# Where the FFN's second bias is added: on GpSimd in the residual, or on TensorE by a matmul with a row of ones

## The chip, the cores and the metric

The kernel runs on one core of one Trainium2 chip. The metric is the device time of one execution in microseconds (us).

## The reference

The reference is a network of four residual parts over x, 16 batches of 256 tokens of 512 values: a long convolution with gating, a mixture of experts, an attention, and a plain FFN. Only the last one is touched:

```
x = x + _L1_ffn_ref(_layernorm(x), proj1, proj1_bias, proj2, proj2_bias, gate_w)
    h   = gelu(einsum('lne,he->lnh', x, proj1) + proj1_bias)      # 512 -> 2048
    out = einsum('lnh,eh->lne', h, proj2) + proj2_bias            # 2048 -> 512
```

The bias `proj2_bias` has 512 values, one for each output column, the same for all 4096 tokens.

## The kernel before

The program is a chain of three phases with a barrier between them: every engine of a phase first waits for all that the phase before has signalled. The first phase (tiles `c_` and `f_` in the trace) does the convolution and the experts, the second (`t_`) the attention, the third (`g_`, function `ffn_phase`) the last FFN. Within a phase each engine works through its own queue strictly in the order in which the program text puts instructions there; `p.do(engine, ..., waits)` adds one and returns a token, and a later instruction on any engine can wait for that token. SyncE (`sync`) issues the loads, GpSimd (`gpsimd`) the stores.

`ffn_phase` works on 8 groups G of 512 tokens (4 tiles t of 128 tokens), and for each group on 16 blocks k of 128 hidden values. All products are made from pairs of rounded parts: a value is split into a high part (`...h`) and a low part (`...l`) of type fp32r, and a product is three matmuls, high by high, low by high, high by low.

- At the start, the four tiles of group 0 are loaded (L986), then the two biases (L990, L991), then the first pair of weight blocks into the two staging buffers `stg` (`fetch(0, 0)`, L1090). `stats`, `norm` and `turn` make the layernorm of a tile (`bn_stats`, `bn_aggr`, a `tensor_scalar` on VectorE, a power on GpSimd, a `tensor_scalar` on VectorE) and transpose it on TensorE into `xh` and `xl`. `place_weights` splits the staged weights into `w1h`, `w1l`, `w2h`, `w2l`, on ScalarE and, for block 0, on GpSimd; later blocks use VectorE.
- `fetch` writes staging buffer i % 2 and waits for `st` and `sth` of i - 2, the two tokens that say that this buffer has been read.
- For each block, `first` makes 12 matmuls of 512 columns into `PH` (L1039), `hidden` the gelu on ScalarE (L1051) and the split into `hh` and `hl` on VectorE (L1052, L1053), and `second`, two blocks later, 12 matmuls of 512 columns (L1062): three for each of the four PSUM banks `O[t]`. A bank gathers over all 16 blocks of its group: the first matmul of block 0 has start=True, the last of block 15 stop=True. The pair `hh`, `hl` has two buffers, taken by the parity of the block.
- `raise_` adds the bias, held as 128 equal rows in `b2s`, to the residual tile `xt` on GpSimd (L1072), four times in a group, at blocks 5, 7, 9 and 11. `evac` then adds `O[t]` on VectorE (L1078) and stores the tile (L1079).
- `second` of block 0 of the next group waits, bank by bank, for that `evac`; `first` of a block stands between them in TensorE's queue.

The buffers of a phase are laid out in SBUF in the order of their `m.sb` calls.

Of the kernel before, what the change touches and what calls it, by code (L numbers as in the profile page):

```python
# [8 lines left out]
F32R = mybir.dt.float32r  # L9
I32 = mybir.dt.int32  # L10
U32 = mybir.dt.uint32
ALU = mybir.AluOpType
ACT = mybir.ActivationFunctionType
# [74 lines left out]
def f32(ap):  # L88
    return ap.bitcast(F32)
# [19 lines left out]
def make_identity(p, ident):  # L109
    a = p.do("gpsimd", lambda e: e.memset(ident, 0.0))  # L110
    return p.do("gpsimd", lambda e: e.affine_select(out=ident, in_=ident, compare_op=ALU.not_equal, fill=1.0, base=0,
                                                    pattern=[[-1, 128]], channel_multiplier=1), a)
# [832 lines left out]
def ffn_phase(nc, ctx, d, before, tag, xin, accs, outs, passes, w1, w2, b1, brow):  # L945
# [3 lines left out]
    NG = 8  # L949
    groups = NG * len(passes)  # L950
    p = Phase(nc, ctx, tag, before)
    m = Mem(nc, ctx, tag)
# [7 lines left out]
    b1s = m.sb("b1s", list(b1.shape))  # L960
    stg = m.sb("stg", [128, 2, 512])

    b2s = m.sb("b2s", [128, 512])
    xt = m.sb("xt", [128, 2, 4, 512])
    ac = m.sb("ac", [128, 4, 512]) if len(passes) > 1 else None
    st = m.sb("st", [128, 2, 6])
    ag = m.sb("ag", [128, 2, 2])
    rs = m.sb("rs", [128, 2, 1])
    xn = m.sb("xn", [128, 2, 512])
# [5 lines left out]
    O = [m.ps(f"O{i}") for i in range(4)]  # L975
    PH = [m.ps(f"PH{i}") for i in range(2)]
    PM = m.ps("PM")
    T = {}

    def g(*k):  # L980
        return T.get(k)
# [4 lines left out]
        T["x0", i] = p.dma("sync", dx0[i], lambda e, i=i: e.dma_start(xt[:, 0, i, :], xin[0][:, i, :]))  # L986
    c_id = make_identity(p, ident)
    c_mh = p.do("gpsimd", lambda e: e.memset(mhalf, -0.5))
    db = p.dsem("bias")
    p.dma("sync", db, lambda e: e.dma_start(b1s[:, :], b1))  # L990
    c_b = p.dma("sync", db, lambda e: e.dma_start(b2s[:, :], brow))  # L991

    da = p.dsem("a")
    dw = [p.dsem(f"w{i}") for i in range(2)]
# [59 lines left out]

    def second(G, k):
        n = G * NB + k
        for t in range(4):
            c = slice(128 * t, 128 * t + 128)
            for q, (a, b_) in enumerate(((hh, w2h), (hl, w2h), (hh, w2l))):
                fin = k == NB - 1 and q == 2  # L1060
                beg = k == 0 and q == 0
                tk = p.do("tensor", lambda e, a=a, b_=b_, t=t, fin=fin, c=c, beg=beg: e.matmul(O[t][:, :], a[:, n % 2, c], b_[:, k, :], start=beg, stop=fin),  # L1062
                          g("hh", n), g("hl", n), g("w2", k), g("add", 4 * (G - 1) + t) if k == 0 else None, inc=(q == 2 and (t == 3 or fin)))
                if fin:
                    T["o", 4 * G + t] = tk
                if q == 2 and t == 3:
                    T["o2", n] = tk

    def raise_(G, t):
        i = 4 * G + t  # L1070
        x = xt[:, G % 2, t, :]
        T["xb", i] = p.do("gpsimd", lambda e: e.tensor_tensor(x, x, b2s[:, :], ALU.add), c_b, g("xn", i))  # L1072

    def evac(G, t):
        i = 4 * G + t
        x = xt[:, G % 2, t, :]
        r = x if G < NG else ac[:, t, :]
        T["add", i] = p.do("vector", lambda e: e.tensor_tensor(x, r, O[t][:, :], ALU.add), g("o", i), g("xb", i))  # L1078
        T["out", i] = p.dma("gpsimd", dout[i % 8], lambda e: e.dma_start(outs[G // NG][G % NG][:, t, :], x), g("add", i))  # L1079

    nst = [0]
# [1 line left out]
    def fetch(G, k):  # L1083

        kb = passes[G // NG][k]
        for src in (w1[kb], w2[kb]):
            i = nst[0]
            nst[0] += 1
            q = stg[:, i % 2, :]
            T["wd", i] = p.dma("sync", dw[i % 2], lambda e, q=q, src=src: e.dma_start(q, src), g("st", i - 2), g("sth", i - 2))  # L1090

    def place_weights(G, k, eng="vector"):

        free = g("o2", (G - 1) * NB + k) if G else None
        i = nst[0] - 2
        ws = ((w1h[:, k, :, :].rearrange("p a b -> p (a b)"), w1l[:, k, :, :].rearrange("p a b -> p (a b)")), (w2h[:, k, :], w2l[:, k, :]))
        for j, (hi, lo) in enumerate(ws):
            T["sth", i + j], T["st", i + j] = split_weight(p, stg[:, (i + j) % 2, :], hi, lo, T["wd", i + j], free, eng)
        T["w1", k], T["w2", k] = T["st", i], T["st", i + 1]
# [30 lines left out]
    for n in range(total + 2):  # L1130
        G, k = divmod(n, NB)
        if n < total:
            if G == 0 and k + 1 < NB:
                place_weights(0, k + 1)
                if k + 2 < NB:
                    fetch(0, k + 2)
            prepare(G, k, 0)
            first(G, k)
            prepare(G, k, 1)
        if n >= 2:  # L1140
            G2, k2 = divmod(n - 2, NB)
            second(G2, k2)
            if (G2 + 1) % NG == 0 and G2 + 1 < groups:

                if k2:
                    place_weights(G2 + 1, k2 - 1)
                fetch(G2 + 1, k2)
                if k2 == NB - 1:
                    place_weights(G2 + 1, k2)
            if k2 in (5, 7, 9, 11):  # L1150
                raise_(G2, (k2 - 5) // 2)
            if k2 == NB - 1:
                for t in range(4):
                    evac(G2, t)
                if G2 + 2 < groups:
                    load(G2 + 2)
                if G2 + 1 < groups:
                    load_acc(G2 + 1)
        if n < total:
            hidden(G, k)  # L1160
# [484 lines left out]
def layouts(inputs):  # L1645

    i = {k: np.asarray(v) for k, v in inputs.items()}
    c = np.ascontiguousarray
    a = {"x": c(i["x"]), "ctx": c(i["ctx_2048"]), "k": c(np.pad(i["L0_xattn_k"], ((0, 0), (128, 0))))}
    ctx = i["ctx_2048"]  # L1650
    a["ctxh"] = c(ctx.reshape(16, 32, 8, 4, 128).transpose(1, 4, 3, 0, 2).reshape(32, 128, 4, 128))
    a["ctxb"] = c(ctx.reshape(16, 256, 4, 128).transpose(0, 3, 2, 1))
    a["skipt"] = c(np.tile(i["fside_S2_0"].reshape(32, 8).T, (16, 1)))
    a["seg"] = c(i["itok_BxS_0_1023"].reshape(16, 2, 128).transpose(0, 2, 1))
    a["rw1"] = c(i["L0_ffn_w1"].reshape(8, 4, 128, 256).transpose(0, 2, 1, 3).reshape(8, 128, 2, 512).transpose(0, 2, 1, 3).reshape(16, 128, 512))
    a["rw2"] = c(i["L0_ffn_w2"].reshape(16, 128, 512))
    a["sw1"] = c(i["L0_ffn_shared_w1"].reshape(4, 128, 4, 128).transpose(2, 1, 0, 3).reshape(4, 128, 512))
    a["sw2"] = c(i["L0_ffn_shared_w2"].reshape(4, 128, 512))
    a["sb1"] = c(i["L0_ffn_shared_b1"].reshape(4, 128).T)
    a["rb1"] = c(i["L0_ffn_b1"])  # L1660
    b2 = np.zeros((96, 512), np.float32)
    for z in (0, 32, 64):
        b2[z:z + 9] = np.concatenate([i["L0_ffn_b2"], i["L0_ffn_shared_b2"][None]])
    a["f0b2"] = b2[:73]
    a["gw"] = c(i["L0_ffn_gate_w"].reshape(4, 128, 8).transpose(1, 0, 2))
    a["f1w1"] = c(i["L1_ffn_proj1"].T.reshape(4, 128, 16, 128).transpose(2, 1, 0, 3).reshape(16, 128, 512))
    a["f1w2"] = c(i["L1_ffn_proj2"].T.reshape(16, 128, 512))
    a["f1b1"] = c(i["L1_ffn_proj1_bias"].reshape(16, 128).T)
    a["f1b2"] = c(np.tile(i["L1_ffn_proj2_bias"], (128, 1)))
    uq, qr, dq, kr = i["L1_xattn_W_uq"], i["L1_xattn_W_qr"], i["L1_xattn_W_dq"], i["L1_xattn_W_kr"]  # L1670
    uqt = uq.T.reshape(16, 128, 192)
    ukt, uvt = [i["L1_xattn_" + n].T.reshape(16, 128, 128) for n in ("W_uk", "W_uv")]
    a["fac"] = c(np.concatenate([uqt, uqt[:, :, 128:], ukt, uvt, i["L1_xattn_W_o"].reshape(16, 128, 512)], -1))
    a["wqra"] = c(qr[:128])
    a["wqrb"] = c(np.concatenate([qr[128:], qr[128:]]))
    a["wkc"] = c(i["L1_xattn_W_kvc"].reshape(4, 128, 128).transpose(1, 0, 2))
    a["wdq"] = c(np.concatenate([dq, dq[:, 128:]], 1).reshape(4, 128, 256).transpose(1, 0, 2))
    sw = np.concatenate([kr[:, 32:], kr[:, :32]], 1)
    a["wkr"] = c(np.stack([np.concatenate([kr, kr], 1), np.concatenate([sw, sw], 1)], 1))
    inv = np.float32(1.0) / np.float32(10000.0) ** (np.arange(32, dtype=np.float32) / np.float32(32))  # L1680
    ang = np.arange(256, dtype=np.float32)[:, None] * inv
    co, si = np.cos(ang).astype(np.float32), np.sin(ang).astype(np.float32)
    co, si = np.concatenate([co, co], 1), np.concatenate([-si, si], 1)
    a["ck"], a["sk"] = c(np.tile(co.T, (2, 1))), c(np.tile(si.T, (2, 1)))
    a["cq"], a["sq"] = c(co.reshape(2, 128, 64).transpose(1, 0, 2)), c(si.reshape(2, 128, 64).transpose(1, 0, 2))
    return a
# [55 lines left out]
```

How the kernel before makes its waits and increments, by code:

```python
    def emit(self, e, eng):  # L69
        seen = {}
        def wait(sem, v):
            if seen.get(id(sem), 0) < v:
                eng.wait_ge(sem, v)
                seen[id(sem)] = v
        for sem, v in self.before:
            wait(sem, v)
        for fn, waits, inc in self.q[e]:
            for w in waits:
                if w is not None:
                    wait(*w)
            ins = fn(eng)
            if inc:
                ins.then_inc(*inc)
# [1635 lines left out]
                def run(eng, e=e):  # L1721
                    for p in phases:
                        p.emit(e, eng)
                    if e == "sync":
                        for sem, v in before:
                            eng.wait_ge(sem, v)
```

## Time and profile before

| | |
|---|---|
| median of 3 runs | 3286.62 us (3286.21 to 3289.66) |
| the profiled execution, one of the three | 3289.66 us |
| its span, first to last instruction | 3287.9 us |
| outside the span | 1.76 us |
| phase 3 in the span | from about 2539 us to the end |
| TensorE busy, whole span | 97% |
| granted TensorE clock, mean | 0.989 of full |

In the profile, L12 means line 12 of the kernel; PE is TensorE, PEld its weight loads, DVE VectorE, ACT ScalarE, POOL GpSimd, SPq the queue of SyncE. A row of the timeline gives the start of an instruction (us from the span's start) and its length. Matmuls are pipelined, so a matmul's length is longer than its distance to the next: what TensorE spends on each is read from start to start.

### The profile page before, as it was taken

Reading aid. Unit: us, or ns where it says so; the run is one execution under the profiler, and the core shown is the slowest. Engines: PE = TensorE matmul, PEld = TensorE weight load, DVE = VectorE, ACT = ScalarE, POOL = GpSimd, SP = SyncE. Lnnn points to the kernel's source line nnn. Section 1 sums busy time; section 2 is a strip of 40 time slices with the busy share of each in tenths; the row PEclk is TensorE's granted clock in tenths of the full one; section 3 lists DMA queues with packets and bytes.
Section 4 is the critical chain, followed back from the end, with each engine's and each line's share of the span. In section 5 each row is a group of like instructions: output and inputs, shape, how many; then the busy total and the mean of one; then the engine's idle time right before and its main releaser. Section 6 shows DMA issues by size and latency. Waiting matters only on the chain.

```text
span 3287.9 us, 51710 instructions
## 1 busy us (share of the span) xinstructions
PE 3176.7 (97%) x18581; PEld 2696.9 (82%) x18581; DVE 2174.6 (66%) x5816; ACT 1267.6 (39%) x3058; POOL 1052.6 (32%) x1114
## 2 busy tenths in 40 slices
PE   7999999999999789999999999999998999999999
PEld 4666666688899679999999999999997788888887
DVE  6888888755555477787878777777876533333332
ACT  2333333233444255555555555555554411111111
POOL 6877777535211222222222222222200111010110
PEclk9999999999999899999999999999999999999999
DMA  4544443259644432111111111111101300000000
GB/s 130 156 135 139 128 143 91 81 168 313 197 152 155 158 116 71 46 46 46 40 40 44 46 46 44 37 45 46 46 14 43 109 26 26 26 26 26 26 14 13
DMA packets 123764, 267.41 MB, mean 81 GB/s; under 512 B 17673, under 2 KB 18321, under 8 KB 123514
## 3 DMA queue, kind: packets, MB, share of 16 engines
q1 hardware_dynamic: 100122, 186.59, 18.1%
q0 software_dynamic: 23392, 77.51, 7.1%
q8 instruction: 153, 2.51, 0.3%
q14 instruction: 97, 0.79, 0.1%
HBM read 159.49 MB, written 104.56 MB: 80 GB/s over the span
## 4 chain that ended last, share of the span: by engine, by line
PE 78%; DVE 10%; POOL 7%; DMA 2%; ACT 1%; issue 1%; SPq 0%; POOLq 0%; DVEq 0%
PE g_PH L1039 11%; PE g_O L1062 11%; PE t_U L1505 10%; PE t_S L1457 9%; PE t_PO L1492 5%; PE t_M L1441 5%; POOL c_kf L354 3%; PE t_T L1479 3%; PE f_Y L916 3%; PE f_Y L386 2%; PE t_M L1396 2%; PE f_Y L687 2%; PE f_Y L381 2%; DVE c_R L399 2%; DVE c_z L393 2%; PE t_M L1378 2%
## 5 line engine op out<-in xcount | busy, mean ns | idle before, releaser
L1467 ACT ACTIVATE t_pr<-t_sm,t_nb 128x256 f32<-128x256 f32 x512 | 256.4, 502 | 369.2 <-DVE t_nb L1463 369.2
L1052 DVE CAST g_hh<-g_hf 128x512 fp32r<-128x512 f32 x128 | 61.8, 482 | 431.4 <-PE g_O L1062 426.8
L1411 POOL TENSOR_TENSOR t_r<-t_r 128x256 f32<-128x256 f32 x128 | 95.7, 748 | 776.0 <-DVE t_rw L1473 457.6
L354 POOL TENSOR_TENSOR c_kf<-c_vt,c_ct 128x512 f32<-128x512 f32 x256 | 296.6, 1179 | 0.2 <-PE f_Y L381 0.2
L1051 ACT ACTIVATE g_hf<-g_PH,g_b1s 128x512 f32<-128x512 f32 x128 | 88.2, 689 | 514.5 <-PE g_PH L1039 514.5
L1474 DVE TENSOR_SCALAR t_pr<-t_pr,t_rw 128x256 f32<-128x256 f32 x512 | 222.2, 434 | 18.2
L386 PE MATMUL f_Y<-c_kh,c_th 128*128 128x512 f32 x448 | 201.1, 449 | 9.2 <-ACT c_kh L361 9.2
L1039 PE MATMUL g_PH<-g_xh,g_w1h 128*128 128x512 f32 x512 | 205.3, 401 | 1.5 <-DVE g_xl L1027 1.5
L1039 PE MATMUL g_PH<-g_xh,g_w1l 128*128 128x512 f32 x512 | 202.9, 396 | 0.0
L1039 PE MATMUL g_PH<-g_xl,g_w1h 128*128 128x512 f32 x512 | 202.6, 396 | 0.0
L1062 PE MATMUL g_O<-g_w2h,g_hh 128*128 128x512 f32 x512 | 202.4, 395 | 0.0
L1505 PE MATMUL t_U<-t_vol,t_oth 128*128 128x512 f32 x512 | 202.3, 395 | 0.0
L1062 PE MATMUL g_O<-g_w2h,g_hl 128*128 128x512 f32 x512 | 202.2, 395 | 0.0
L1505 PE MATMUL t_U<-t_voh,t_otl 128*128 128x512 f32 x512 | 202.0, 395 | 0.0
L1062 PE MATMUL g_O<-g_w2l,g_hh 128*128 128x512 f32 x512 | 201.5, 394 | 0.0
L1505 PE MATMUL t_U<-t_voh,t_oth 128*128 128x512 f32 x512 | 200.9, 392 | 0.0
L1463 DVE CUSTOM_DVE_ANT_0 t_sm<-t_S,t_mk 128x256 f32<-128x256 f32 x512 | 194.8, 418 | 7.7 <-PE t_S L1457 7.7
L393 DVE TENSOR_TENSOR c_z<-f_Y,c_ct 128x512 f32<-128x512 f32 x256 | 174.1, 680 | 37.2 <-PE f_Y L381 37.0
L381 PE MATMUL f_Y<-c_kf,c_t 128*128 128x512 f32 x384 | 186.4, 594 | 0.0
L1484 DVE TENSOR_TENSOR t_ptl<-t_T,t_pth 128x512 fp32r<-128x512 f32 x256 | 175.6, 686 | 15.5 <-ACT t_pth L1483 15.4
L399 DVE TENSOR_REDUCE c_R<-c_z 128x64 f32<-128x512 f32 x256 | 175.0, 683 | 6.6
L386 PE MATMUL f_Y<-c_kh,c_tl 128*128 128x512 f32 x448 | 178.2, 398 | 0.0
(355 smaller groups left out, 9695.1 us busy)
## 6 DMA issues: line engine op xcount, KB each, us to landing
xs<-c_zero SPq DMA_DIRECT2D x71, 256.0 KB, 5.2
f_xg<-xs SPq DMA_DIRECT2D x71, 256.0 KB, 2.8
ys<-f_yt POOLq DMA_DIRECT2D x71, 256.0 KB, 2.4
c_tr<-kpad SPq DMA_DIRECT2D x60, 256.0 KB, 4.8
f_xg<-xn SPq DMA_DIRECT2D x40, 256.0 KB
c_xt<-x SPq DMA_DIRECT2D x32, 256.0 KB, 3.5
c_cr<-ctx SPq DMA_DIRECT2D x32, 256.0 KB, 3.9
c_ct<-ctxh SPq DMA_DIRECT2D x32, 256.0 KB, 4.3
```

Of the source, the lines that this page charges most:

```text
L354: T["kv", h] = T["kv1", n] = p.do("gpsimd", lambda e: e.tensor_tensor(o, iv, ic, ALU.mult), g("vt", h), g("ct", h), g("kl", n - 8), g("kh" ...
L381: last = p.do("tensor", lambda e, c=c, mb=mb: e.matmul(Y[y % 4][:, :], t0[:, s, c], kf[:, v, mb, :], start=False, stop=mb == lb), g("t0", ...
L386: last = p.do("tensor", lambda e, a=a, b_=b_, c=c, mb=mb, i=i: e.matmul(Y[y % 4][:, :], a[:, s, c], b_[:, v, mb, :], start=(mb == 0 and i ...
L393: T["z", h] = T["z1", y] = p.do("vector", lambda e: e.tensor_tensor(zz.rearrange("p (b j i) -> p b j i", i=8, j=8), iv, ic, ALU.mult), las ...
L399: T["red", y] = T["R", h] = p.do("vector", lambda e: e.tensor_reduce(rr, zr, AXX, ALU.add), g("z1", y), g("pr", h - 2))
L1039: T["ph", n] = p.do("tensor", lambda e, kk=kk, a=a, b_=b_, i=i: e.matmul(ph[:, :], a[:, k, kk, :], b_[:, s, kk, :], start=i == 0, stop=i = ...
L1062: tk = p.do("tensor", lambda e, a=a, b_=b_, t=t, fin=fin, c=c, beg=beg: e.matmul(O[t][:, :], a[:, n % 2, c], b_[:, k, :], start=beg, stop= ...
L1457: a = p.do("tensor", lambda e, t=t, j=j, q=q, k=k: e.matmul(PS1[:, 256 * t:256 * t + 256], q, k[:, s, :], start=j == 0, stop=j == 4), g("q ...
L1463: T["am", N] = am = p.do("vector", lambda e, t=t, k4=k4: e.tensor_tensor_reduce(out=sm[:, k4, :], in0=PS1[:, 256 * t:256 * t + 256], in1=m ...
L1467: T["ex", x] = p.do("scalar", lambda e, t=t, k4=k4: e.activation(pr[:, N % 2, t, :], sm[:, k4, :], ACT.Exp, bias=nb[:, k4, 0:1], scale=-1. ...
L1474: T["nm", x] = p.do("vector", lambda e, t=t, k4=k4: e.tensor_scalar(pr[:, N % 2, t, :], pr[:, N % 2, t, :], rw[:, k4, 1:2], None, ALU.mult ...
L1505: a = p.do("tensor", lambda e, t=t, tt=tt, j=j, o=o, w=w: e.matmul(PU[t][:, :], o[:, N % 3, tt], w[:, h, :], start=h == 0 and j == 0, stop ...
```

## The change

The bias leaves the residual. It becomes one more matmul in front of each PSUM bank's sum: the stationary operand is `oner` (33 rows by 128 columns, ones in rows 0 and 32, zeros between), the moving operand `br` (33 rows by 512 columns, row 0 the bias's high part, row 32 its low part). The host now hands over 33 rows, zeros but for rows 0 and 32, instead of 128 equal rows. They are loaded into the first staging buffer, rounded to fp32r on ScalarE (`c_bh`), and row 32 is replaced by the remainder on VectorE (`c_br`). As the staging buffer is shared with the weights, the tokens of these two become `sth` and `st` of index -2, on which the first `fetch` waits. `oner` is made by three memsets on GpSimd and a copy on VectorE. The four adds of `raise_` in a group go, and `evac` waits for what `raise_` had waited for.

```diff
-    b2s = m.sb("b2s", [128, 512])
+    KB = 33
+    BL = slice(32, 33)
+    brs = stg[0:KB, 0, :]
+    br = m.sb("br", [KB, 512], F32R)
...
+    ones = m.sb("ones", [33, 128])[:, :]
+    oner = m.sb("oner", [33, 128], F32R)[:, :]
+    a = p.do("gpsimd", lambda e: e.memset(ones, 0.0))
+    for z in (0, 32):
+        a = p.do("gpsimd", lambda e, z=z: e.memset(ones[z:z + 1, :], 1.0), a)
+    c_on = p.do("vector", lambda e: e.tensor_copy(oner, ones), a)
     db = p.dsem("bias")
     p.dma("sync", db, lambda e: e.dma_start(b1s[:, :], b1))
-    c_b = p.dma("sync", db, lambda e: e.dma_start(b2s[:, :], brow))
+    c_b = p.dma("sync", db, lambda e: e.dma_start(brs, brow))
+    c_bh = p.do("scalar", lambda e: e.activation(br[:, :], brs, ACT.Copy), c_b)
+    c_br = p.do("vector", lambda e: e.tensor_tensor(br[BL, :], brs[BL, :], f32(br[BL, :]), ALU.subtract), c_bh, c_b)
+    T["sth", -2], T["st", -2] = c_bh, c_br
...
     def second(G, k):
         n = G * NB + k
+        bias = G // NG == len(passes) - 1
         for t in range(4):
             c = slice(128 * t, 128 * t + 128)
+            if k == 0 and bias:
+
+                p.do("tensor", lambda e, t=t: e.matmul(O[t][:, :], oner, br[:, :], start=True, stop=False),
+                     c_on, c_br, g("add", 4 * (G - 1) + t), inc=False)
             for q, (a, b_) in enumerate(((hh, w2h), (hl, w2h), (hh, w2l))):
                 fin = k == NB - 1 and q == 2
-                beg = k == 0 and q == 0
+                beg = k == 0 and q == 0 and not bias
...
-    def raise_(G, t):
-        i = 4 * G + t
-        x = xt[:, G % 2, t, :]
-        T["xb", i] = p.do("gpsimd", lambda e: e.tensor_tensor(x, x, b2s[:, :], ALU.add), c_b, g("xn", i))
-
     def evac(G, t):
...
-        T["add", i] = p.do("vector", lambda e: e.tensor_tensor(x, r, O[t][:, :], ALU.add), g("o", i), g("xb", i))
+        T["add", i] = p.do("vector", lambda e: e.tensor_tensor(x, r, O[t][:, :], ALU.add), g("o", i), g("x", G), g("a", G), g("xn", i))
...
-            if k2 in (5, 7, 9, 11):
-                raise_(G2, (k2 - 5) // 2)
...
-    a["f1b2"] = c(np.tile(i["L1_ffn_proj2_bias"], (128, 1)))
+    b2 = np.zeros((33, 512), np.float32)
+    b2[0], b2[32] = i["L1_ffn_proj2_bias"], i["L1_ffn_proj2_bias"]
+    a["f1b2"] = b2
```

## Rows read from the trace of the kernel before

**Rows 1.** Stretches of the last phase: us, busy and count per engine, PEclk, DMA share, GB/s.
```profile
2534.00:2554.03 20.03, 4.85 (x19) 3.12 (x19) 10.86 (x23) 4.14 (x8) 6.36 (x10) 0.57 0.50 170
2554.03:3282.25 728.22, 728.22 (x3184) 589.04 (x3184) 252.19 (x457) 123.57 (x186) 72.51 (x90) 1.00 0.09 30
```

**Rows 2.** Timeline of TensorE, two `second` blocks: start, length, instruction.
```profile
2564.04 0.40 PE L1062 MATMUL g_O<-g_w2h,g_hh 128*128 128x512 f32 x1
...
2566.80 0.39 PE L1039 MATMUL g_PH<-g_xh,g_w1h 128*128 128x512 f32 x1
...
2569.60 0.40 PE L1062 MATMUL g_O<-g_w2h,g_hh 128*128 128x512 f32 x1
...
2572.40 0.39 PE L1039 MATMUL g_PH<-g_xh,g_w1h 128*128 128x512 f32 x1
```

**Rows 3.** Tile g_xt: the adds that the change removes; length ns min/median/max.
```profile
L1072 POOL TENSOR_TENSOR g_xt<-g_xt,g_b2s x32: 1275/1293/1464, 2594.4 to 3204.1; 128x512 f32<-128x512 f32 x32
```

**Rows 4.** Who waited for whom from 2600 us on: us in total, times, longest.
```profile
DVE g_xt L1078 <- PE g_O L1062: 18.1, 8, 2.3
```

**Rows 5.** Timeline, phase 1: a matmul with 73 rows of contraction between ones with 128.
```profile
864.16 0.39 PE L687 MATMUL f_Y<-c_sw,f_hh 128*128 128x512 f32 x1
864.39 0.40 PE L683 MATMUL f_Y<-f_br,f_gT 73*128 73x512 f32 x1
864.63 0.39 PE L687 MATMUL f_Y<-c_sw,f_hh 128*128 128x512 f32 x1
```

**Rows 6.** The chain that ended last, at the last phase's start: start, length, what.
```profile
2539.61 2.68 DMA g_xt<-x
...
2542.41 0.70 DVE g_st L117
...
2554.03 10.17 PE g_PH L1039 x36
```

**Rows 7.** Timeline of the last phase's start, all engines.
```profile
2539.61 1.76 SPq L986 DMA_DIRECT2D g_xt<-x  x4
...
2541.41 0.43 SPq L990 DMA_DIRECT2D g_b1s<-f1b  x1
2541.88 0.43 SPq L991 DMA_DIRECT2D g_b2s<-f1b  x1
2542.36 8.31 SPq L1090 DMA_DIRECT2D g_stg<-f1w  x4
...
2546.91 0.62 ACT L105 ACTIVATE g_w1h<-g_stg 128x512 fp32r<-128x512 f32 x1
...
2552.61 0.60 ACT L1026 ACTIVATE g_xh<-g_O 128x512 fp32r<-128x512 f32 x1 [1.64 <-PE g_O L1021]
...
2553.24 0.69 DVE L1027 TENSOR_TENSOR g_xl<-g_O,g_xh 128x512 fp32r<-128x512 f32 x1 [1.24 <-ACT g_xh L1026]
```

**Rows 8.** DMA issues of that start: KB each, us to landing.
```profile
g_xt<-x SPq DMA_DIRECT2D x1, 256.0 KB, 4.4
g_b2s<-f1b SPq DMA_DIRECT2D x1, 256.0 KB, 4.1
g_stg<-f1w SPq DMA_DIRECT2D x1, 256.0 KB, 4.3
g_b1s<-f1b SPq DMA_DIRECT2D x1, 8.0 KB, 3.7
```

**Rows 9.** Timeline, phase 1: the same kind of bias split, and a copy to fp32r.
```profile
19.12 0.63 ACT L422 ACTIVATE f_br<-f_stg 73x512 fp32r<-73x512 f32 x1 [3.13 <-DMA f_stg<-f0b]
...
20.13 0.68 DVE L423 TENSOR_TENSOR f_br<-f_stg,f_br 9x512 fp32r<-9x512 f32 x1
...
22.16 0.23 DVE L428 CAST c_one<-c_onef 128x128 fp32r<-128x128 f32 x1 [1.36 <-POOL c_onef L427]
```

**Rows 10.** Timeline of TensorE before and where its granted clock rises in this phase.
```profile
2556.73 0.63 PE L1039 MATMUL g_PH<-g_xh,g_w1h 128*128 128x512 f32 x1
2557.16 0.48 PE L1039 MATMUL g_PH<-g_xh,g_w1l 128*128 128x512 f32 x1
```

## The prediction

> **What bounds the kernel now.** I read the page's busy shares first: TensorE is busy 97% of the span, which is an average over three phases and says little of this one. The change lives in the last phase alone, so I read the stretches of that phase. From its first block matmul at 2554.03 us to its last one at 3282.25 us TensorE is busy for all of 728.22 us, with 3184 matmuls, while VectorE is busy for 252 us, ScalarE for 124 and GpSimd for 73 [rows 1]. That is busy time by modelled ends, so I checked it start to start. 3072 of the 3184 are block matmuls of 512 columns, 112 are transposes. One group of twelve takes 2566.80 - 2564.04 = 2.76 us, another 2572.40 - 2569.60 = 2.80 us [rows 2], so a matmul costs 0.230 or 0.233 us of TensorE's time, although each row gives it a length near 0.39. 3072 x 0.232 = 713 us; the remaining 15 us are 28 sets of four transposes (about 0.45 each, 13 us) and a slow beginning, and that is the whole stretch. There is no stall left in it: TensorE sets the end, and each matmul put into its queue there moves the end by its start-to-start time.
>
> The other place where this phase can lose time is its start. From 2534.00 to 2554.03 us TensorE is busy for 4.85 us of 20.03 at half its clock (PEclk 0.57) [rows 1]. There the chain that ended last leaves TensorE: it runs from the load of the first tile over the first `bn_stats` at 2542.41, VectorE's and GpSimd's small steps, and transposes to the first block matmul at 2554.03 [rows 6]. What delays VectorE there delays everything.
>
> **The change part by part.**
>
> *Removed adds.* 32 adds on GpSimd of 1.293 us each (41 us) go [rows 3]. GpSimd has 72.5 us of work in 728 [rows 1], and the only instruction behind the adds, `evac`'s add on VectorE, idles for TensorE's last matmul of a bank and for nothing else (18.1 us, 8 times) [rows 4]. Gain on the path: 0. If this cover were gone, by GpSimd being late, the row of waits would name GpSimd; it doesn't.
>
> *Added matmuls.* Eight groups times four banks are 32 matmuls with 512 columns and 33 rows of contraction, each with its weight load. This phase has no such shape. Phase 1 has one with 73 rows between matmuls of 128 rows: 864.39 - 864.16 = 0.23 us before it and 864.63 - 864.39 = 0.24 behind it [rows 5]. It costs what a full matmul costs; fewer rows save nothing, and the change of shape loses nothing. 32 x 0.233 = 7.5 us. The bounds: in proportion to the rows, 33/128 of that, 1.9 us; or the full shown length, 0.396 each (the row says 0.40), 12.7 us, if the pipeline drained at each. I take 7.5, since row 864.39 is nearly the same thing. The waits of these matmuls cost nothing: `oner` and `br` are ready some 20 us earlier, and the wait for the add on the same bank is the one that the first matmul of a bank had, covered by the 2.8 us of `first` in front of it.
>
> The Trainium skill's page "TensorE: Matmul & The Clock Gate", section "Back-to-back issue gap", gives a sustained spacing of about 131 ns for a matmul of 512 columns in a stream with weight loads; this trace shows 233 ns in the same kind of stream, with fp32r operands. By the skill's figure the 32 would cost an estimated 4.2 us and the whole change an estimated 8.4; the row decides.
>
> *The start.* This is what I think is easily missed. `c_br`, the subtraction that makes the bias's low part, stands in VectorE's queue ahead of `stats(0)`, and it waits for `c_bh` on ScalarE, which waits for the bias's load. Queues are in order, so the first `bn_stats`, which could begin at 2542.41 because its tile had landed at 2542.29 (2539.61 + 2.68) [rows 6], now stands behind the bias. Before, nothing at the start waited for the bias: its first reader was the gelu.
> When does the bias land? The loads are issued in order: the four tiles, b1s at 2541.41, the bias at 2541.88, the weights at 2542.36 [rows 7]. The last of the four tiles, issued at about 2539.61 + 1.76 - 0.43 = 2540.9 [rows 7], took 4.4 us and landed at about 2545.3; b1s landed at 2541.41 + 3.7 = 2545.1, the bias of 256 KB at 2541.88 + 4.1 = 2546.0 [rows 8]. The new one is 33 rows of 2 KB, 66 KB, behind the same megabyte of tiles; `c_b` counts both biases. I take 2545.2, near b1s; bounds 2544.2 (if the tiles land a microsecond earlier because no weights follow close behind) and 2546.0 (no earlier than the large one).
> Then `c_bh`: 0.63 us, as for the 73-row bias [rows 9]; about 0.03 us from ScalarE's end to VectorE's start, as from 2552.61 + 0.60 to 2553.24 [rows 7]; `c_br`: 0.68 us, as for 9 rows [rows 9]; and 0.05 us to the first `bn_stats`, together 1.4 us. So `bn_stats` begins at 2546.6 instead of 2542.41: 4.2 us later. Bounds: 2544.2 + 1.4 gives 3.2; 2546.0 + 1.4 and a slower hand-over (in phase 1 VectorE began 20.13 - 19.75 = 0.38 us after ScalarE had ended [rows 9]) give 5.4.
> Do the weights become a second delay? SyncE holds `fetch(0, 0)` until `c_br` has ended, since it writes the same staging buffer, and with it everything behind it in SyncE's queue: both weight blocks, `fetch(0, 1)` and the next group's tile load. Before, the fetch was issued at 2542.36, 0.05 us before the first `bn_stats`, and ScalarE first used a weight block 4.5 us after that `bn_stats`, at 2546.91 [rows 7], when it had just landed (2542.36 + 4.3) [rows 8]. After, it is issued at the same moment relative to `bn_stats`, with no tiles ahead of it, so it lands no later relative to the chain. Both shift together: no extra cost. Without that cover the ScalarE queue, in which the next tile's `xh` stands behind the weights, would pass it on one for one.
> The three memsets on GpSimd fall into its idle time before the first `rs`, and the copy of 33 x 128 on VectorE (a 128 x 128 one took 0.23 us [rows 9]) into VectorE's idle time until the tile or the bias lands: 0.
> The rise of the clock moves along with the stream. At 2556.73 matmuls are 0.43 us apart, and the fast level (2.4 GHz for 1.2) comes at about 2557.3, some 3.3 us into the dense stream [rows 10]. Relative to the stream it may come earlier or later by chance: 8 matmuls at the slow level cost 8 x 0.2 = 1.6 us now, so I allow 1.5 us either way and expect 0.
>
> *Elsewhere.* `br` takes the place of `b2s` (2 KB in each partition both) and `oner` comes behind all other buffers, so no other buffer moves. The end behind 3282.25 is unchanged.
>
> *Sum.* 0 + 7.5 + 4.2 = 11.7 us. The profiled execution took 3289.66 us (span 3287.9 and 1.76 outside), so such an execution would take 3301.4. It was the slowest of three and lies 3.04 us above their median; against the median of 3286.62 the forecast is 3298.3 us, 0.36% slower. No change that can be measured means within 0.2% of the median, 6.6 us: 3280.0 to 3293.2.
>
> **Rivals.**
>
> *The start is free.* The bias would land early enough, or other work would catch up the delay before 2554.03. For it: VectorE idles in that start. Against: no block of idle time follows the first `bn_stats`, where the chain runs almost without a wait [rows 6]. It gives 3286.62 + 7.5 = 3294.1, hardly slower than the bound.
>
> *Each odd-shaped matmul drains the pipeline.* Then 12.7 + 4.2 = 16.9 us, 3303.5. Against it, the 0.24 us behind the 73-row matmul [rows 5].
>
> *Few rows are cheap.* 1.9 + 4.2 = 6.1 us, 3292.7, no measurable change. The same row speaks against it.
>
> *The added matmuls slip in at a lower spacing.* By the distance that a fully pipelined stream would allow, if the added ones, which all load the same 33 rows and stream the same `br`, ran at half of the present 0.233 us: 3.7 + 4.2 = 7.9 us, 3294.5. Against: in 728 us of stream the mean never falls there, and the groups of twelve in [rows 2], three to a bank, show 0.230 at the least. The Trainium skill's spacing of about 131 ns, cited above, is the rule that stands beside this case.
>
> *The other side: the stream itself gets faster.* Of the groups of twelve some take 2.76 us, others 2.80, and in `second` this goes by the parity of the block, so by which buffer of `hh` and `hl` is read [rows 2]. If the change moved buffers or access patterns so that the 128 groups of `first` and the 64 slow ones of `second` all ran at 2.76, it would give back 192 x 0.035 = 6.7 us: 11.7 - 6.7 = 5.0, 3291.6, not slower by my bound. It decides from 5.1 us of 6.7 on. Against: the buffers stay where they are.
>
> **How the numbers follow.** The forecast 0.75; free start 0.10; drain 0.05; cheap rows 0.03; lower spacing 0.03; faster stream 0.04. Bounds of the forecast's own terms: 7.4 + 3.2 - 1.5 = 9.1 and 7.5 + 5.4 + 1.5 = 14.4, 3295.7 to 3301.0. Runs of the same kernel spread by 3.5 us, so I widen to 3302.0 above. Below, the range takes in the free start and the lower spacing, 3293.5. Slower by over 0.2%: the forecast, drain, lower spacing and half of the free start, 0.88. Within: the other half, cheap rows and three quarters of the faster stream, 0.11. Faster: 0.01.
>
> **What the profile after would show.** 3216 matmuls in the stream, 32 of them with the form 33 x 512 and their next start 0.23 us on; VectorE's `bn_stats` beginning about 4.2 us later than before, with a wait for ScalarE in front of `c_br`, and the first block matmul about as much later; the first weight load issued behind it; no GpSimd adds; `evac`'s wait still for TensorE. I would be wrong if the barrier of the phase or the tiles' landing shifted too, if the row of the 33-row matmul showed 0.4 us to its next, or if the odd and even groups of twelve no longer took 2.80 and 2.76.

## The result, and the profile after

The changed kernel takes 3311.16 us (median of 6 runs, 3310.03 to 3315.59) against 3286.36 us (6 runs, 3285.16 to 3289.66) before: ratio 1.0075, 95% interval 1.0064 to 1.0086. It is slower by 24.8 us. The forecast was 3298.3 us, 11.7 us more than before, with a range to 3302.0: the sign was right, the size was half of the real one.

The profiled execution of the changed kernel is not one of these six; it took 3308.17 us, with a span of 3306.4. That is 18.5 us more than the profiled one before, not 24.8, because in it the two earlier phases, whose code is the same, ended 5.8 us sooner: the first tile load of the last phase was issued at 2533.80 us instead of 2539.61 [rows 7]. Measured from that load to the end of the span, the last phase took 3287.9 - 2539.61 = 748.3 us before and 3306.4 - 2533.80 = 772.6 us after. The difference, 24.3 us, is the one of the medians, and this is the measure to compare profiles by here. That the two agree within half a microsecond is partly chance: the start alone varies by more than that from profile to profile, as the experiments show.

First the stretches of the last phase, the start and the stream of block matmuls (us, busy and count of PE, PEld, DVE, ACT, POOL, then PEclk, DMA share, GB/s), as in [rows 1]:

```profile
2533.40:2552.93 19.53, 4.17 (x16) 2.92 (x17) 10.41 (x23) 4.77 (x9) 6.14 (x12) 0.50 0.44 138
2552.93:3301.00 748.07, 747.96 (x3216) 592.68 (x3216) 238.69 (x458) 123.84 (x186) 32.34 (x58) 1.00 0.09 29
```

The stream has its 32 more matmuls, 3216, and all but 0.1 us of it is busy by this view, at full clock. It begins at 2552.93 and its last matmul starts at 3300.49, 747.56 us later; before, from 2554.03 to 3282.02, it was 727.99 (the prediction's 3282.25 is the end of its stretch). So 19.6 us of the 24.3 came in the stream. Divided by 32 this is 0.61 us for each added matmul, where I had put down 0.233.

The timeline of TensorE and its weight loads around one of them, the second bias matmul of a group:

```profile
2657.90 0.40 PE L1079 MATMUL g_O<-g_w2l,g_hh 128*128 128x512 f32 x1
2658.23 0.18 PEld L1074 LDWEIGHTS g_O<-g_br,g_oner 33*128 33x128 f32 x1 [0.36 <-issue]
2658.23 0.50 PE L1074 MATMUL g_O<-g_br,g_oner 33*128 33x512 f32 x1
2658.65 0.19 PEld L1079 LDWEIGHTS g_O<-g_w2h,g_hh 128*128 128x128 f32 x1 [0.24 <-issue]
2658.66 0.50 PE L1079 MATMUL g_O<-g_w2h,g_hh 128*128 128x512 f32 x1
2658.76 0.19 PEld L1079 LDWEIGHTS g_O<-g_w2h,g_hl 128*128 128x128 f32 x1
2659.00 0.39 PE L1079 MATMUL g_O<-g_w2h,g_hl 128*128 128x512 f32 x1
```

Read the PE rows from start to start: 0.33 us from the matmul before to the bias matmul, 0.43 to the next, 0.34 to the one behind that, and then 0.23 again. Now read the PEld rows. Elsewhere in the stream a weight load begins together with the matmul before it and is over when that ends. Here the bias's weight load begins only with its own matmul, 0.33 us after the one before had begun, and so does the load behind it. Two loads in a row have lost their cover, and the third, at 2658.76, begins 0.10 us later than the matmul that should cover it. The means over all 32 are 0.326, 0.427 and 0.34 us, 1.09 us for three distances, of which two were there before: the price is 1.09 - 2 x 0.232 = 0.63 us, 32 x 0.63 = 20.2 us. The stream grew by 19.6, a little less, and two small things lie between: the clock rose about 0.4 us later in this execution (below), and of the undisturbed groups of twelve in `second` only 38 of 117 took 2.80 us instead of 2.76, where before it was 61 of 125, which gives back about 0.8 us.

The matmul's own length is 0.497 us, by the view of the tile g_br (min/median/max in ns), but a sum made from the lengths would not have found 0.63 either, because a part of it falls on the neighbours:

```profile
L1074 PE MATMUL g_O<-g_br,g_oner x32: 492/497/498, 2563.5 to 3221.7; 33*128 33x512 f32 x32
```

The start, in the chain that ended last (start, length, what):

```profile
2536.08 3.81 DMA g_stg<-f1b
...
2540.00 0.64 ACT g_br L1001
2540.66 0.68 DVE g_br L1002
2541.37 0.71 DVE g_st L117
...
2552.93 10.60 PE g_PH L1051 x36
```

In [rows 6] the chain went from the tile's load straight to `g_st L117`. Now it goes through the bias's load, `c_bh` (L1001) and `c_br` (L1002). The first `bn_stats` begins 2541.37 - 2533.80 = 7.57 us behind the first tile load, before 2542.41 - 2539.61 = 2.80: 4.8 us later. The first block matmul begins 19.13 us behind that load, before 14.42: 4.7 us later.

The removed adds: `evac`'s wait for TensorE is the same as in [rows 4].

```profile
DVE g_xt L1090 <- PE g_O L1079: 18.1, 8, 2.3
```

### The profile page after: what moved, and what is told of

Same layout as the page of the kernel before. It is cut to its first block, busy times and chain, and to the rows that moved or that the text cites. A ratio compares the mean times of both kernels' runs of the same rounds, so it can differ in the third digit from the quotient of the medians.

```text
span 3306.4 us, 51716 instructions
## 1 busy us (share of the span) xinstructions
PE 3190.9 (97%) x18613; PEld 2698.1 (82%) x18613; DVE 2164.9 (65%) x5818; ACT 1269.4 (38%) x3059; POOL 1014.3 (31%) x1085
## 4 chain that ended last, share of the span: by engine, by line
PE 79%; DVE 10%; POOL 7%; ACT 1%; DMA 1%; issue 1%; SPq 0%; POOLq 0%; DVEq 0%; ACTq 0%
PE g_PH L1051 11%; PE g_O L1079 11%; PE t_U L1515 10%; PE t_S L1467 9%; PE t_PO L1502 5%; PE t_M L1451 5%; POOL c_kf L354 3%; PE t_T L1489 3%; PE f_Y L916 3%; PE f_Y L687 2%; PE f_Y L386 2%; PE t_M L1406 2%; PE f_Y L381 2%; DVE c_R L399 2%; DVE c_z L393 2%; PE t_M L1388 2%
## 5 line engine op out<-in xcount | busy, mean ns | idle before, releaser
L1064 DVE CAST g_hh<-g_hf 128x512 fp32r<-128x512 f32 x128 | 55.0, 429 | 481.8 <-PE g_O L1079 476.8
```

## The experiments

The two theories that I took into them. For the stream: the shape of the new matmul is at fault (A), or its place in front of a bank and its waits (B). For the start: the bias's split at the head of VectorE's queue, or something else in the set-up. The times below come from two later sessions, each with the kernel before on the same chip: 3286.97 us for the runs "65 rows", "four together", "start alone" and "split moved", 3286.42 us for "64 rows", "32 rows", "adds alone" and "both repairs". The ratios are taken within a session. Where a run is set against the changed kernel's 3311.16 us, measured with 3286.36 us before, the comparison crosses sessions, and up to 0.6 us of it is the sessions' own difference.

**65 rows instead of 33.**

```diff
-    KB = 33
-    BL = slice(32, 33)
+    KB = 65
+    BL = slice(64, 65)
```

with `ones`, `oner` and the host's array of 65 rows to match, ones and bias in rows 0 and 64.

> The bias matmul with 65 rows of contraction instead of 33 (ones in rows 0 and 64, the low part in row 64, zeros between); nothing else. Theory A (shape): at 64 rows or fewer the array works in a narrower arrangement, and going into and out of it costs 0.63 us per bias matmul; 65 rows behave like the 73 rows of the first phase: 0.23 us to the next start, weight load under the matmul before, so 32 x (0.63 - 0.23) = 12.8 us off the changed kernel, about 3298.4 us. Rival B (place): it is dear because it opens a PSUM bank or because of its waits, whatever its rows: it stays at 0.33 + 0.43 us and the time at about 3311.

3298.69 us (5 runs), ratio 1.0039, interval 1.0025 to 1.0053. Theory A, to 0.3 us; 12.5 us below the changed kernel. The profiles say the same of the stream, from the first block matmul to the last: 735.4 us against 747.6. The timeline around a bias matmul:

```profile
2659.71 0.40 PE L1051 MATMUL g_PH<-g_xl,g_w1h 128*128 128x512 f32 x1
2659.72 0.19 PEld L1074 LDWEIGHTS g_O<-g_br,g_oner 65*128 65x128 f32 x1
2659.95 0.40 PE L1074 MATMUL g_O<-g_br,g_oner 65*128 65x512 f32 x1
2659.95 0.19 PEld L1079 LDWEIGHTS g_O<-g_w2h,g_hh 128*128 128x128 f32 x1
...
2660.18 0.40 PE L1079 MATMUL g_O<-g_w2h,g_hh 128*128 128x512 f32 x1
```

Both weight loads lie under the matmul before them again, and the distances are 0.24 and 0.23 us. The matmul stands at the same place, opens the same bank and has the same waits: B falls.

**64 rows.** The same edit with 64 rows, ones and bias in rows 0 and 32.

> The bias matmul with 64 rows (ones in rows 0 and 32, zeros between and behind). Theory A puts the border between 64 and 65 rows: 0.33 us before and 0.43 behind each bias matmul, as with 33 rows. If the cost grew smoothly as rows fall, or had to do with 33 as an odd number, 64 rows would show 0.23 or something between; one run, about 3311 against about 3299.

3313.48 us in one run.

```profile
2661.91 0.40 PE L1051 MATMUL g_PH<-g_xl,g_w1h 128*128 128x512 f32 x1
2662.23 0.18 PEld L1074 LDWEIGHTS g_O<-g_br,g_oner 64*128 64x128 f32 x1 [0.37 <-issue]
2662.24 0.49 PE L1074 MATMUL g_O<-g_br,g_oner 64*128 64x512 f32 x1
...
2662.66 0.19 PEld L1079 LDWEIGHTS g_O<-g_w2h,g_hh 128*128 128x128 f32 x1 [0.24 <-issue]
```

0.33 and 0.42 us, as with 33 rows; the means over the 32 are 0.326 and 0.427. Between 64 rows and 65 there is a step, not a slope. The single total, 2.3 us above the changed kernel's median, says no more than that; the distances carry the reading.

**32 rows.** One one, the high part alone, no subtraction.

```diff
-    KB = 33
+    KB = 32
...
-    c_br = p.do("vector", lambda e: e.tensor_tensor(br[BL, :], brs[BL, :], f32(br[BL, :]), ALU.subtract), c_bh, c_b)
+    c_br = c_bh
```

> The bias matmul with 32 rows: only row 0 holds a one and the bias's high part; the low part and its subtraction on VectorE are left out. By theory A the same price as with 33 rows or near it: the stream leaves the 128-row arrangement just the same, 0.33 and 0.43 us. If the narrowest shape were cheaper, its distance to the next would be under 0.43. The start is some 0.7 us shorter for want of the subtraction: about 3310.5 by theory A.

3304.23 us in one run, where 3310.5 was expected. The distances are what A says:

```profile
2655.03 0.50 PE L1073 MATMUL g_O<-g_br,g_oner 32*128 32x512 f32 x1
2655.46 0.19 PEld L1078 LDWEIGHTS g_O<-g_w2h,g_hh 128*128 128x128 f32 x1 [0.24 <-issue]
```

0.43 us to the next, and a mean of 0.425 over the 32. The stream takes 747.4 us, as in the changed kernel. The total lies 6 us lower than expected, and part of that is the start, which I had misjudged. Without the subtraction nothing at the head of VectorE's queue waits for the bias any more:

```profile
2532.07 1.76 SPq L988 DMA_DIRECT2D g_xt<-x  x4
...
2534.70 0.69 DVE L117 BATCH_NORM_STATS2 g_st<-g_xt 128x6 f32<-128x512 f32 x1 [1.01 <-DMA g_xt<-x]
...
2538.35 0.63 ACT L1000 ACTIVATE g_br<-g_stg 32x512 fp32r<-32x512 f32 x1 [13.51 <-DMA g_stg<-f1b]
...
2539.01 6.24 SPq L1101 DMA_DIRECT2D g_stg<-f1w  x4
...
2541.68 0.63 ACT L105 ACTIVATE g_w1h<-g_stg 128x512 fp32r<-128x512 f32 x1 [2.22 <-DMA g_stg<-f1w]
```

The first `bn_stats` is back at 2.63 us behind the first tile load, and what is late now is the weight fetch (L1101), which still waits for `c_bh`. ScalarE waits 2.22 us for those weights, and the chain that ended last goes from there over the low parts on GpSimd to the first block matmul, 2548.61 - 2532.07 = 16.5 us behind the load: 2.6 us sooner than in the changed kernel, 2.1 us later than before. From the first load to the end it took 3301.9 - 2532.07 = 769.8 us against 772.6, which is this difference. So the bias holds up two queues side by side; the fetch alone would cost 2.1 us, and in the changed kernel it is hidden behind the late `bn_stats`. The rest of the 6 us lies ahead of this phase, in one execution: its first tile load was issued at 2532.07 us, sooner than in any other profile.

**The four bias matmuls of a group together.**

```diff
+        for t in range(4 if k == 0 and bias else 0):
+            p.do("tensor", lambda e, t=t: e.matmul(O[t][:, :], oner, br[:, :], start=True, stop=False),
+                 c_on, c_br, g("add", 4 * (G - 1) + t), inc=False)
         for t in range(4):
             c = slice(128 * t, 128 * t + 128)
-            if k == 0 and bias:
-
-                p.do("tensor", lambda e, t=t: e.matmul(O[t][:, :], oner, br[:, :], start=True, stop=False),
-                     c_on, c_br, g("add", 4 * (G - 1) + t), inc=False)
```

> The four bias matmuls of a group stand one behind the other ahead of the twelve others of block 0 instead of one ahead of each three; 33 rows as before. Theory A1 (only the switch costs): one way in and one way out per group instead of four; the three inner distances fall from 0.43 to 0.23 us; 8 x (4 x 0.63 - (0.09 + 3 x 0.23 + 0.43 + 0.11)) = 9.6 us off, about 3301.6. Theory A2 (the narrow matmul itself streams at half rate): inner distances 0.43, 8 x (2.52 - (0.09 + 4 x 0.43 + 0.11)) = 4.8 us off, about 3306.4. Rival B (the bank's opening costs): no gain, 3311.

3300.72 us (4 runs), ratio 1.0047, interval 1.0030 to 1.0063: 10.4 us off the changed kernel, A1 had said 9.6, A2 4.8. The stream takes 737.4 us, 10.1 less. In the timeline the four are one row:

```profile
2656.86 0.40 PE L1051 MATMUL g_PH<-g_xl,g_w1h 128*128 128x512 f32 x1
2657.18 1.20 PE L1071 MATMUL g_O<-g_br,g_oner 33*128 33x512 f32 x4
2658.31 0.50 PE L1078 MATMUL g_O<-g_w2h,g_hh 128*128 128x512 f32 x1
2658.65 0.40 PE L1078 MATMUL g_O<-g_w2h,g_hl 128*128 128x512 f32 x1
```

Narrower windows of the same timeline leave out the first of the four, the first two, the first three, and so show where the others start; below them are the weight loads behind the four:

```profile
2657.52 0.86 PE L1071 MATMUL g_O<-g_br,g_oner 33*128 33x512 f32 x3
2657.75 0.62 PE L1071 MATMUL g_O<-g_br,g_oner 33*128 33x512 f32 x2
2657.99 0.39 PE L1071 MATMUL g_O<-g_br,g_oner 33*128 33x512 f32 x1
...
2658.31 0.19 PEld L1078 LDWEIGHTS g_O<-g_w2h,g_hh 128*128 128x128 f32 x1 [0.37 <-issue]
2658.42 0.19 PEld L1078 LDWEIGHTS g_O<-g_w2h,g_hl 128*128 128x128 f32 x1
```

The distances are 0.32 into the new shape, then 0.34, 0.23, 0.24, then 0.32 back to 128 rows and 0.34 behind that. Over all eight groups the means are 0.327, 0.340, 0.232, 0.232, 0.323 and 0.342. So a matmul of 33 rows isn't slow: between its like it is 0.23 us apart, the speed of the 128-row stream. What costs is each change of shape, and it costs at two places, about 0.09 us at the first matmul of the new shape, whose weights load only with it, and about 0.11 at the second, whose weights load 0.11 us late. The 0.43 us behind a lone bias matmul is both at once, the second place of the way in and the first of the way out: 0.232 + 0.11 + 0.09. One visit costs 0.32 + 1.13 + 0.34 - 2 x 0.232 = 1.33 us with four matmuls in it, of which 4 x 0.233 = 0.93 is their own time: 0.40 us for a way in and out, as for a lone matmul, 0.63 - 0.23.

**The start alone.** The changed kernel without its bias matmuls; the bias is not added.

```diff
-            if k == 0 and bias:
-
-                p.do("tensor", lambda e, t=t: e.matmul(O[t][:, :], oner, br[:, :], start=True, stop=False),
-                     c_on, c_br, g("add", 4 * (G - 1) + t), inc=False)
...
-                beg = k == 0 and q == 0 and not bias
+                beg = k == 0 and q == 0
```

> The bias matmuls are left out (the bias is then not added at all); the split at the start, the shared staging buffer and the removed adds stay as in the changed kernel. It shows the start's price alone. If the start costs 4.7 us (the profile after has the first block matmul that much later behind the first load) and the removed adds give nothing: 3286.4 + 4.7 = 3291.1. If the removed adds on GpSimd give TensorE something back, less. If the start is free: 3286.4.

3291.51 us (10 runs), ratio 1.0015, interval 1.0005 to 1.0025: 4.5 us for the start, as expected, though the interval alone would allow anything from 1.6 to 8.2. The profile is narrower: from the first tile load to the end 3289.3 - 2537.08 = 752.2 us against 748.3 before, 3.9 us, with the first block matmul 18.5 us behind the load instead of 14.4. Among the profiles with the split at the head of the queue (33, 64 and 65 rows, four together, and this one) that delay lies between 4.1 and 5.4 us.

**The split moved behind the first block.**

```diff
-    brs = stg[0:KB, 0, :]
...
+    brs = m.sb("brs", [KB, 512])[:, :]
...
-    c_bh = p.do("scalar", lambda e: e.activation(br[:, :], brs, ACT.Copy), c_b)
-    c_br = p.do("vector", lambda e: e.tensor_tensor(br[BL, :], brs[BL, :], f32(br[BL, :]), ALU.subtract), c_bh, c_b)
-    T["sth", -2], T["st", -2] = c_bh, c_br
...
+        if n == 0:
+            c_bh = p.do("scalar", lambda e: e.activation(br[:, :], brs, ACT.Copy), c_b)
+            c_br = p.do("vector", lambda e: e.tensor_tensor(br[BL, :], brs[BL, :], f32(br[BL, :]), ALU.subtract), c_bh, c_b)
         if n < total:
             hidden(G, k)
```

The new staging buffer lies behind all others, and the split stands between the first block's matmuls and its gelu.

> The bias gets a staging buffer of its own behind all others, and its split on ScalarE and VectorE stands behind the first block instead of ahead of the layernorm; the weight fetch no longer waits for it. 33 rows and all 32 bias matmuls stay. My theory (VectorE's and SyncE's queues held up by the bias): the first bn_stats begins again 2.8 us behind the first load, and 4.7 us go, about 3306.5. Rival (the start is later for another reason, such as the tiles' landing or the additional set-up work): the start stays 19.1 us from the first load to the first block matmul and the time stays at 3311.

3306.62 us (4 runs), ratio 1.0063, interval 1.0046 to 1.0080: 4.5 us off the changed kernel. The timeline of its start:

```profile
2536.72 1.76 SPq L988 DMA_DIRECT2D g_xt<-x  x4
2538.52 0.43 SPq L999 DMA_DIRECT2D g_b1s<-f1b  x1
2539.00 0.39 SPq L1000 DMA_DIRECT2D g_brs<-f1b  x1
...
2539.45 0.69 DVE L117 BATCH_NORM_STATS2 g_st<-g_xt 128x6 f32<-128x512 f32 x1 [0.85 <-DMA g_xt<-x]
...
2551.20 0.77 PE L1048 MATMUL g_PH<-g_xh,g_w1h 128*128 128x512 f32 x1 [1.46 <-DVE g_xl L1036]
```

`bn_stats` waits for its tile again and begins 2.73 us behind the first load (2.80 before); the first block matmul 14.48 us behind it (14.42 before). The memsets and the copy for `oner` are still there, so they cost nothing. This edit frees the weight fetch too, so it removes both of the waits that the run with 32 rows tells apart.

**The removed adds alone.** As the one above, and no bias matmuls; the bias is not added.

> Only the 32 adds on GpSimd are gone: no bias matmuls, and the split of the bias stands behind the first block with a staging buffer of its own (the bias is not added at all). My step: the adds were covered by TensorE's work and their removal gives 0: 3286.7, ratio 1.000. Rival: GpSimd's traffic slowed VectorE or TensorE, and its removal gives back some us: under 3283.

3287.21 us (11 runs), ratio 1.0004, interval 0.9995 to 1.0013. No difference that can be seen; the interval leaves room for a gain of 1.6 us and a loss of 4.3. The profile closes it further: from the first tile load to the end it is 3285.5 - 2537.33 = 748.2 us, against 748.3 with the adds. The adds were covered.

**Both repairs.** 65 rows and the late split.

> The change with both repairs: 65 rows of contraction, and the split of the bias behind the first block with its own staging buffer. Left is the plain price of 32 matmuls at 0.233 us: 3286.7 + 7.5 = 3294.2, ratio 1.0023. If the two repairs shared a cause, more than that would remain; if the removed adds gave something back, less.

3293.75 us (11 runs), ratio 1.0023, interval 1.0014 to 1.0032. This is the idea of the change at its plain price, 7.3 us above the kernel before by these medians, where 32 x 0.233 = 7.5 was expected; the interval is 4.6 to 10.5. In the profile the stream takes 736.4 us, 8.4 more than before, and 0.9 of that lies in its first 36 matmuls, among which the clock rose later (10.9 us against 10.0), so 7.5 are left. It doesn't beat the kernel before, and nothing in these runs points to a version that would: the work taken away is worth nothing, and TensorE has no gap to put a matmul in.

## Why the prediction was wrong

- *TensorE sets the end; each matmul put into its queue moves it.* Right. Of the changed kernel's 24.8 us 12.5 go with the shape, 4.5 with the split, and what is left, 7.8, is about the 7.3 of the kernel with both repairs. By the differences within each session it is 13.1, 5.1 and 6.6, so the shares are good to about a microsecond.
- *Removed adds: 0.* Right on the path, shown by the run without adds and matmuls. VectorE did lose time to them, which the wait of `evac` doesn't show (last section).
- *Added matmuls: 7.5 us.* This is the step that failed: "It costs what a full matmul costs; fewer rows save nothing, and the change of shape loses nothing", and "I take 7.5, since row 864.39 is nearly the same thing". The first half is right: in a row of four, the third and the fourth 33-row matmul each start 0.23 us behind the one before. The second is wrong. A 73-row matmul between 128-row ones [rows 5] is not a nearby case of a 33-row one: between 64 and 65 rows lies a step, and 73 is on the side of 128. The term measured 32 x 0.63 = 20.2 us. I should have asked which property of a shape makes its neighbours' weight loads fit under it, and not by how many rows it differed.
  The upper bound was too low for a second reason. I took the shown length, 0.396 us, as the most that a drained pipeline could cost; 12.7 us. But the price falls on three distances, and two of them end in matmuls that aren't new: the successor, whose weights load only with it, and the one behind that, whose weights load late. The rival "each odd-shaped matmul drains the pipeline" was the right mechanism with 12.7 where 20.2 belonged, so 3303.5 where 3311.2 came; I had given it 0.05. The sign that I had named for being wrong, 0.4 us from the 33-row matmul to its next, is what the profile shows.
  The Trainium skill's page "TensorEngine Tiling (Array Packing)" has the rule that I did not weigh. Its section "Available Configurations" gives row tilings of 64 and of 32 rows beside the untiled 128, and "Key Properties" says that changing the mode drains TensorE. The runs agree: 32, 33 and 64 rows behave alike and 65 like 73 and 128, and the price comes once for each way in and out. The page gives no price; here it is 0.40 us a visit. That it is the tiling mode which changes, and that TensorE drains, is the page's account; the runs show the border and the lost cover of the loads.
- *The start: 4.2 us.* Right in its mechanism, and near in size: 4.7 us in the profile, 4.5 by the medians, inside the bounds of 3.2 and 5.4 (the five profiles reach from 4.1 to 5.4). The part that was short is the landing of the bias, for which I took 2545.2 - 2541.88 = 3.3 us after its issue; it took 3.81. From there to `bn_stats` it was 1.4 us, as worked out. The later weight fetch cost nothing more, as predicted: the time from `bn_stats` to the first block matmul was 11.62 us before and 11.56 after. That holds only while `bn_stats` is late too; with 32 rows, where it isn't, the fetch costs 2.1 us by itself.
- *The rise of the clock.* As before within a matmul or two: the 0.23 us distances begin 2557.48 - 2554.03 = 3.45 us behind the first block matmul before, 2557.28 - 2552.93 = 4.35 after. Two more matmuls pass at the slow level, which is 0.4 us of time. In the other profiles it is up to seven more (64 rows), 1.3 us, inside the 1.5 that I had allowed.
- *The range.* Its upper end, 3302.0, stands on the forecast's 7.5 us for the matmuls, 5.4 for the start, 1.5 for the clock and a little spread. The bound of 12.7 is not in it; that stood only in the rival, whose 3303.5 lies outside.

## What to carry to other kernels

A price read from a neighbouring shape holds only if nothing changes kind between the two. Before borrowing a matmul's cost for another number of rows, see whether both lie on the same side of 64, where the step lay here (fp32r operands, 512 columns), and if the nearest row lies on the other, keep the change of shape as the upper bound and count it at two matmuls on each way. If a narrow matmul has to stand in a stream of full ones, pad it with zero rows to more than 64, or put all narrow ones together. A small set-up step at the head of an in-order queue can cost its whole wait for its load; put it where the engine is idle and its result is still early. Look then for a second queue that waits for the same step, as the weight fetch did here: freeing one alone gave back only part.

## What the runs showed of the hardware

The rows of contraction beyond the ones needed are free, and here even save time: 65 rows cost 0.24 us to the next start, 33 rows 0.43, with the same 512 columns.

GpSimd's adds did hold up VectorE, though TensorE lost nothing by it. The group of the split's first cast, from the page, of the kernel before and then of the changed one (busy, mean ns, idle before):

```profile
L1052 DVE CAST g_hh<-g_hf 128x512 fp32r<-128x512 f32 x128 | 61.8, 482 | 431.4 <-PE g_O L1062 426.8
```

```profile
L1064 DVE CAST g_hh<-g_hf 128x512 fp32r<-128x512 f32 x128 | 55.0, 429 | 481.8 <-PE g_O L1079 476.8
```

482 ns on the mean with the adds, 429 without, and 429 too in the run with the adds alone removed. The mean hides what happens: 121 of the 128 casts took 429 ns before as well, and the seven that ran while an add did took 1.38 to 1.42 us. All seven can be read like this one:

```profile
2698.49 1.41 DVE L1052 CAST g_hh<-g_hf 128x512 fp32r<-128x512 f32 x1 [3.25 <-PE g_O L1062]
```

The add beside it ran from 2698.33 to 2699.61, and the cast ended at 2699.90, some 0.3 us after it. In all seven the cast ended that long after the add that was running when it began. It looks as if VectorE stood still until the add was over. The subtraction behind the cast shows it at its worst, when it met four adds in a row:

```profile
3199.93 6.03 DVE L1053 TENSOR_TENSOR g_hl<-g_hf,g_hh 128x512 fp32r<-128x512 f32 x1
3200.38 5.03 POOL L1072 TENSOR_TENSOR g_xt<-g_xt,g_b2s 128x512 f32<-128x512 f32 x4
```

Its usual length is 0.69 us. In all, casts and subtractions took 13 us less without the adds, and all of it became idle time. It would have cost time had TensorE been waiting for VectorE.

The groups of twelve matmuls of `second` went on taking 2.76 or 2.80 us, 2.76 more often than before, and several blocks in a row. So it isn't the parity of the buffer alone, as I had put it in the last rival; it wasn't strictly so before either, where blocks in a row took 2.76 in the first group. What decides it was not tried.
